# The last two query heads projected inside the first four attention steps

## The chip, the cores and the metric

The kernel runs on one core of one Trainium2 chip. The core has a matrix engine (TensorE, PE in the profile), a vector engine (VectorE, DVE), a scalar engine (ScalarE, ACT), a general engine (GpSimd, POOL) and an engine that here only issues DMA transfers (SyncE, SP). Each runs its own list of instructions in order, and they wait for each other by semaphores. The metric is the device time of one execution in microseconds (us); lower is better.

## The reference

Two layers over a batch of 8 sequences of 112 rows and width 1024, with a context of 375 rows for each sequence. Only the second layer's attention matters here. All of it is float32.

```python
x = x + attention0(layernorm(x), ctx)          # single head, 1024 wide
x = x + ffn0(layernorm(x))                      # routed low-rank experts
# second layer: grouped attention, 32 query heads of 128 in 8 groups of 4
q = apply_rope((layernorm(x) @ wq).reshape(8, 112, 32, 128).transpose(0, 2, 1, 3), pos)
k = apply_rope(ctx @ wk ...)                    # 8 key heads
v = ctx @ wv ...                                # 8 value heads
attn = softmax(q @ k.T / sqrt(128) + mask)
x = x + (attn @ v).reshape(8, 112, 4096) @ wo
x = x + ffn1(layernorm(x))
```

## The kernel before

Every float32 product is made of three TensorE passes over operands that were split into a high and a low part (`split_product`, L202 in the rows). ACT makes the high part, POOL or DVE subtracts it from the raw data to get the low part.

The kernel is a row of phases, each one a block with its own list for every engine, and a block ends with a barrier of all engines. Two phases matter.

**The query phase** (`query1_phase`, from L1071) projects the 32 query heads in 16 pairs. A pair has 4 units (head t of 0 and 1, half h of the 896 tokens). A unit is 24 matmuls of 128x448 into one PSUM bank. DVE then rotates it by the position tables: three products that read the bank (L736 to L738) and one addition of two buffers in SBUF (L1209, into `q_rotated_then_x_rows`), and SP stores it to memory. The weights of the next pair are loaded (L1126), split by ACT (L1162) and by POOL (L1180) in two slots. Units are counted from 0 to 63; the last pair has 60 to 63. Between these last four units stand the first pieces of the attention: the scores of step 0, their masking, exponentials and normalisation. The mask (1312.5 KB) and the first tiles (q and k of steps 0 and 1, v of step 0) are loaded by SP in front of weights of the last pair. A q tile has 224 KB, k 188, v 187.5, a head's weights 512, so this burst has 2836 KB.

**The attention phase** (`attention_phase`, from L1392) has 64 steps, one for each group of 4 heads and each sequence (step s, sequence u = s mod 8, group g = s div 8), written out one after the other. In step s the engines do:

- PE: scores of step s+1 for heads 0 and 1 (6 matmuls), 12 transposes of the normalised scores of step s (L1564), output projection of an earlier step, first half (`project`, 12 matmuls), scores of step s+1 for heads 2 and 3, second half of the projection (12 matmuls), and the product with v (9 matmuls). The projections of steps 0 to 3 don't exist: nothing is finished yet.
- DVE: masks and row maxima of heads 0 and 1 of step s+1 (L1343, L1347), low parts of the three transposed tiles (L1515), the first addition to `y_t` (L1505), masks of heads 2 and 3, the second addition, reciprocal and four scalings (`normalise`, L1360 and L1363, SBUF to SBUF), low part of the output (L1527, `e_o_t_low`).
- ACT: high parts of q and k of step s+2, of the three transposed tiles, exponentials of step s+1, high part of v of step s+1 (L1313), high part of the output (L1461).
- POOL: low parts of q and k of step s+2 (L1319), of v of step s+1 (L1324), in the first half of each group the low part of a tile of the output weights (L1481), and in steps 0 to 3 a memset of a quarter of `y_t` (L1484).

The order on each engine is written by hand. PE starts the transposes of a step only when DVE has normalised that step (`normed`), and `project` of step s waits for the low part of the output of step s - u mod 4 - 1 (`o_low`).

The last phase (`final_phase`) loads 1084 KB of constants and five rows tiles of 448 KB, each issued by SP behind the last v tile.

## Time and profile before

| | |
|---|---|
| Median of 3 runs | 1939.86 us (1935.42 to 1948.66) |
| The profiled execution, whole time | 1937.03 us |
| Its span from the first to the last instruction | 1935.2 us |
| Mean granted TensorE clock | 0.985 of full speed |
| PE busy | 1852.1 us, 96% |
| DVE busy | 1105.3 us, 57% |
| ACT and POOL busy | 627.5 and 622.7 us, 32% each |

Times in the rows are us from the start of the span. "Busy" of PE counts a matmul that runs at a lower clock for its full length. A row with x4 is four instructions merged, with the time from the start of the first to the end of the last.

### The profile page before, as it was taken

How to read it: one execution, taken by the hardware profiler on the slowest of the kernel's cores; microseconds unless marked ns; L12 is line 12 of the kernel's file. 1: busy time of each engine (PE TensorE's matmuls, PEld its weight loads, DVE VectorE, ACT ScalarE, POOL GpSimd, SP SyncE). 2: the span in 40 equal slices, each digit the busy share in tenths (PEclk: the TensorE clock that was granted, in tenths of full speed). 3: DMA queues.
4: the chain of work that ended last, by engine and by line, in shares of the span. 5: the costliest groups of instructions: out<-in, count | busy, mean ns of one | idle time of the engine just before them, and what ended most of it. 6: DMA issues, size and time to landing. Idle time of an engine off the chain costs nothing. (4 is left out here: it accounts for less than half of the span.)

```text
span 1935.2 us, 27961 instructions
## 1 busy us (share of the span) xinstructions
PE 1852.1 (96%) x9628; PEld 1666.0 (86%) x9628; DVE 1105.3 (57%) x2473; ACT 627.5 (32%) x1337; POOL 622.7 (32%) x427
## 2 busy tenths in 40 slices
PE   5999999999999999989999998799999999999996
PEld 5998999998677777768999997699999999999984
DVE  6631465554222222235666665877777777777766
ACT  2211211112222222221111112656666566665612
POOL 2323432225222222212222222634434344343413
PEclk9999999999999999999999999899999999999999
DMA  4112432345333333312222224333323233233403
GB/s 121 55 55 76 146 110 91 99 142 150 118 115 114 114 114 113 100 53 85 98 101 98 102 99 143 96 84 86 99 74 97 84 86 99 74 97 84 126 10 96
DMA packets 137965, 188.98 MB, mean 98 GB/s; under 512 B 41320, under 2 KB 107432, under 8 KB 137872
## 3 DMA queue, kind: packets, MB, share of 16 engines
q1 hardware_dynamic: 137872, 187.80, 31.6%
q8 instruction: 52, 0.85, 0.2%
q14 instruction: 41, 0.34, 0.1%
HBM read 141.14 MB, written 46.63 MB: 97 GB/s over the span
## 5 line engine op out<-in xcount | busy, mean ns | idle before, releaser
L202 PE MATMUL bank<-shared_operand_high,w_first_high 128*128 128x448 f32 (+1 forms) x768 | 279.5, 364 | 15.8 <-issue 4.8
L202 PE MATMUL bank<-shared_operand_high,w_first_low 128*128 128x448 f32 (+1 forms) x768 | 278.8, 363 | 0.0
L202 PE MATMUL bank<-shared_operand_low,w_first_high 128*128 128x448 f32 (+1 forms) x768 | 278.7, 363 | 0.0
L1354 ACT ACTIVATE e_scores<-e_scores,e_nmax 112x375 f32<-112x375 f32 x256 | 155.0, 610 | 126.1 <-DVE e_nmax L1347 120.9
L202 PE MATMUL bank<-e_o_t_high,e_wo_high 128*128 128x448 f32 x512 | 192.5, 376 | 1.3 <-DVE e_o_t_low L1527 1.3
L202 PE MATMUL bank<-e_o_t_high,e_wo_low 128*128 128x448 f32 x512 | 187.3, 366 | 0.0
L202 PE MATMUL bank<-e_o_t_low,e_wo_high 128*128 128x448 f32 x512 | 186.7, 365 | 0.0
L279 POOL TENSOR_TENSOR shared_operand_low<-ctx_raw,shared_operand_high 128x752 fp32r<-128x752 f32 x64 | 116.4, 1831 | 210.3 <-ACT shared_operand_high L275 210.3
L202 PEld LDWEIGHTS bank<-shared_operand_high,w_first_high 128*128 128x128 f32 x768 | 145.9, 190 | 27.9 <-issue 5.3
L202 PEld LDWEIGHTS bank<-shared_operand_low,w_first_high 128*128 128x128 f32 x768 | 145.9, 190 | 9.7
L202 PEld LDWEIGHTS bank<-shared_operand_high,w_first_low 128*128 128x128 f32 x768 | 145.7, 190 | 9.8
L1343 DVE CUSTOM_DVE_ANT_0 e_scores<-bank,e_mask 112x375 f32<-112x375 f32 x256 | 139.9, 546 | 12.1 <-PE bank L202 3.0
L1180 POOL TENSOR_TENSOR w_first_low<-aw_weights_then_ctx_rows,w_first_high 128x1024 fp32r<-128x1024 f32 x30 | 72.4, 2414 | 224.4 <-ACT w_first_high L1162 224.4
L1505 DVE TENSOR_TENSOR y_t<-bank,y_t 128x448 f32<-128x448 f32 x128 | 80.0, 625 | 107.3 <-PE bank L202 107.2
L1324 POOL TENSOR_TENSOR e_v_low<-e_raw_v,e_v_high 125x384 fp32r<-125x384 f32 x64 | 65.1, 1017 | 235.6 <-ACT e_v_high L1313 235.6
L202 PE MATMUL bank<-shared_operand_high,w_rest_low 128*128 128x376 f32 x384 | 128.5, 335 | 0.0
L202 PE MATMUL bank<-shared_operand_low,w_rest_high 128*128 128x376 f32 x384 | 128.4, 334 | 0.0
L202 PE MATMUL bank<-shared_operand_high,w_rest_high 128*128 128x376 f32 x384 | 127.9, 333 | 0.2 <-POOL w_rest_low L677 0.2
L275 ACT ACTIVATE shared_operand_high<-ctx_raw 128x752 fp32r<-128x752 f32 x64 | 52.2, 829 | 219.6 <-DMA ctx_raw<-in_ctx_t 201.1
L1162 ACT ACTIVATE w_first_high<-aw_weights_then_ctx_rows 128x1024 fp32r<-128x1024 f32 x30 | 31.8, 1061 | 261.3 <-PE bank L202 242.2
L202 PE MATMUL bank<-w_rest_high,shared_operand_high 128*125 128x512 f32 x288 | 114.2, 396 | 0.0
L202 PE MATMUL bank<-w_rest_low,shared_operand_high 128*125 128x512 f32 x288 | 113.7, 395 | 0.0
(173 smaller groups left out, 4214.8 us busy)
## 6 DMA issues: line engine op xcount, KB each, us to landing
ctx_raw<-in_ctx_t SPq DMA_DIRECT2D x64, 376.0 KB, 3.7
e_raw_wo<-in_wo SPq DMA_DIRECT2D x32, 512.0 KB, 5.5
aw_weights_then_ctx_rows<-in_wq SPq DMA_DIRECT2D x30, 512.0 KB, 3.6
q_rotated<-q_rotated_then_x_rows SPq DMA_DIRECT2D x64, 224.0 KB, 1.9
e_raw_q<-q_rotated SPq DMA_DIRECT2D x64, 224.0 KB, 2.8
k_rotated<-k_rotated_sb SPq DMA_DIRECT2D x64, 188.0 KB, 1.9
e_raw_k<-k_rotated SPq DMA_DIRECT2D x64, 188.0 KB, 2.9
aw_weights_then_ctx_rows<-in_ctx_nat SPq DMA_DIRECT2D x8, 1500.0 KB
```

Of the source, the lines that this page charges most:

```text
L202: mm = pe.matmul(out, stationary[a], moving[b], start=(first and i == 0), stop=(last and i == 2))
L275: act.activation(k.ctx_ring[0][slot][:, 2 * j:2 * j + 2, :], k.c_raw[:, j % 2], ACT.Copy).then_inc(done, 1)
L279: pool.tensor_tensor(k.ctx_ring[1][slot][:, 2 * j:2 * j + 2, :], k.c_raw[:, j % 2], f32(k.ctx_ring[0][slot][:, 2 * j:2 * j + 2, :]), ALU.s ...
L1162: act.activation(k.w_first[0][:, t], k.raw[:, t], ACT.Copy).then_inc(w_high, 1)
L1180: pool.tensor_tensor(k.w_first[1][:, t], k.raw[:, t], f32(k.w_first[0][:, t]), ALU.subtract).then_inc(w_low, 1)
L1324: pool.tensor_tensor(self.v[1][:, t], self.raw_v[:, t], f32(self.v[0][:, t]), ALU.subtract).then_inc(self.v_low, 1)
L1343: dve.tensor_tensor_reduce(self.s_buf[:, t, h, :], self.s_bank[h % 2][0:SEQ, 0:KEYS], self.mask[:, u, :], 1.0, LOWEST, ALU.add, ALU.max, s ...
L1354: act.activation(self.s_buf[:, t, h, :], self.s_buf[:, t, h, :], ACT.Exp, bias=self.nm[:, t, h:h + 1], accum_out=self.total[:, t, h:h + 1] ...
L1505: dve.tensor_tensor(k.yt[:, tile, at:at + HALF], y_bank[t][:, 0:HALF], k.yt[:, tile, at:at + HALF], ALU.add).then_inc(y_added, 1)
```

## The change

1. The query phase and the attention phase are one block. The barrier between them is gone. Since buffers of both phases now live at the same time, their places in SBUF are laid out by hand: the attention's buffers lie over those of the query phase in an order that lets each be free when it is needed, and the buffers of the last phase (`ln4`, `lora1`, `tri1_sb`) are carved out of the mask's region.
2. The pair loops end one pair earlier. The pieces of attention step 0 now stand between the units of pair 14 (units 56 to 59). The units 60 to 63 are projected one in each of the attention steps 0 to 3, in two halves of 12 matmuls, in the places where later steps have the output projection. Their banks are the two of the output projection. DVE rotates such a unit at the end of the step, after `normalise` and ahead of the low part of the output. SP stores it in the next step.
3. The split of the weights of the last pair moves: the high part of tile 0 goes ahead of the exponentials of step 0, that of tile 1 behind them, and both low parts behind the first q, k and v splits on POOL.
4. The mask is loaded after the first pair's stores, and the first q, k and v tiles one pair earlier, behind the weights.
5. The output weights of group 0 are split in steps 3 to 6 and not 0 to 3. The memsets of `y_t` are gone; the additions of steps 4 to 11 are copies.
6. The loads of the last phase's constants and rows wait until all masks have been read (`first.masked` at 256).

```diff
-            query1_phase(nc, k, first)
-            layer0.close()
-            attention_phase(nc, k, first)
+            with nc.Block() as block:
+                last_heads = query1_phase(nc, k, first, layer0, heads, block)
+                layer0.close()
+                attention_phase(nc, k, first, last_heads, heads, block)
...
+    def bank_of(i, t, h):
+        return bank[2 + h] if known(i) and i == LAST else bank[2 * t + h]
...
+        for unit, (t, h) in enumerate(FIRST):
+            store(unit, 0, t, h)
+        first.load_mask(sp)
...
+        first.split_high(act)
+        weight_high(LAST, 0, 4 * LAST + 2)
+        first.exps(act, 0, 0, range(PER_GROUP))
+        weight_high(LAST, 1, 4 * LAST + 4)
...
+        first.split_low(pool)
+        weight_low(LAST, 0)
+        weight_low(LAST, 1)
...
+    def products_of_last(pe, n, part):
+        if part == 0:
+            pe.wait_ge(w_low, 2 * LAST + n // 2 + 3)
+            pe.wait_ge(read, 4 * LAST + n + 3)
+            products(pe, LAST, n // 2, n % 2, range(CH // 2))
+        else:
+            products(pe, LAST, n // 2, n % 2, range(CH // 2, CH)).then_inc(acc, 1)
...
+            if s < FILLED:
+                last_heads.rotate(dve, s)
+            dve.wait_ge(o_high, s + 1)
...
+            if s < FILLED:
+                last_heads.products(pe, s, 0)
+            else:
+                project(s, u, 0)
...
     @block.sync
     def _(sp):
+        sp.wait_ge(first.masked, 4 * GROUPS * BATCH)
         for dst, src in ((aw, k.a1), (tri, k.tri1)):
```

**The order on PE** at the start of step 0. Before (`e_q` and `e_k` are the split q and k of a step, `e_p_t` the transposed probabilities):

```order
L1564 MATMUL bank<-ident,e_scores 125x112 x12
L202 MATMUL bank<-e_k_high,e_q_high 112x376
L202 MATMUL bank<-e_k_low,e_q_high 112x376
L202 MATMUL bank<-e_k_high,e_q_low 112x376
L202 MATMUL bank<-e_k_high,e_q_high 112x376
L202 MATMUL bank<-e_k_low,e_q_high 112x376
L202 MATMUL bank<-e_k_high,e_q_low 112x376
L202 MATMUL bank<-e_p_t_high,e_v_high 128x448
```

Now (`shared_operand` is the normalised input, `w_first` the query weights):

```order
L1660 MATMUL bank<-ident,e_scores 125x112 x12
L203 MATMUL bank<-shared_operand_high,w_first_high 128x448
L203 MATMUL bank<-shared_operand_low,w_first_high 128x448
L203 MATMUL bank<-shared_operand_high,w_first_low 128x448
L203 MATMUL bank<-shared_operand_high,w_first_high 128x448
L203 MATMUL bank<-shared_operand_low,w_first_high 128x448
```

Twelve projection matmuls stand between the transposes and the next scores, and twelve more behind those scores.

**The order on DVE** at the end of step 0. Before:

```order
L1360 RECIPROCAL e_inv<-e_total 112x4
L1363 TENSOR_SCALAR e_scores<-e_scores,e_inv 112x375 x4
L1527 TENSOR_TENSOR e_o_t_low<-bank,e_o_t_high 128x4x112
L1343 ISA e_scores,e_max<-bank,e_mask 112x375
L1343 ISA e_max 112x1
```

Now:

```order
L1417 RECIPROCAL e_inv<-e_total 112x4
L1420 TENSOR_SCALAR e_scores<-e_scores,e_inv 112x375 x4
L738 TENSOR_TENSOR q_straight<-bank,q_rope 128x448
L739 TENSOR_TENSOR q_crossed<-bank,q_rope 64x448
L740 TENSOR_TENSOR q_crossed<-bank,q_rope 64x448
L1211 TENSOR_TENSOR q_rotated_then_x_rows<-q_straight,q_crossed 128x448
L1620 TENSOR_TENSOR e_o_t_first_low<-bank,e_o_t_first_high 128x4x112
L1400 ISA e_scores,e_max<-bank,e_mask_then_layer_ffn 112x375
```

The four operations of the rotation stand between the scaling of one step and the first mask of the next.

**The order on SP** where the loop over pairs ends. Before:

```order
L1140 COMPARE_AND_BRANCH
L1368 DMA e_mask<-in_mask 112x8x375
L1288 DMA e_raw_q<-q_rotated 128x4x112
L1291 DMA e_raw_k<-k_rotated 128x376
L1288 DMA e_raw_q<-q_rotated 128x4x112
L1291 DMA e_raw_k<-k_rotated 128x376
L1296 DMA e_raw_v<-v_rows 125x3x128
L1126 DMA raw_weights_then_ctx_rows<-in_wq 128x1024
```

Now:

```order
L1130 COMPARE_AND_BRANCH
L1122 DMA raw_weights_then_ctx_rows<-in_wq 128x1024
L1345 DMA e_raw_q<-q_rotated 128x4x112
L1348 DMA e_raw_k<-k_rotated 128x376
L1345 DMA e_raw_q<-q_rotated 128x4x112
L1348 DMA e_raw_k<-k_rotated 128x376
L1353 DMA e_raw_v<-v_rows 125x3x128
L1116 DMA q_rotated<-q_rotated_then_x_rows 128x448 x2
```

The weights stand first, and the mask is not in this place at all.

## Rows read from the trace of the kernel before

**Rows 1.** The page, busy time of PE: us, share, instructions.

```profile
PE 1852.1 (96%) x9628; PEld 1666.0 (86%) x9628; DVE 1105.3 (57%) x2473; ACT 627.5 (32%) x1337; POOL 622.7 (32%) x427
```

**Rows 2.** Waits of PE, 1150 to 1265: total us, times, longest.

```profile
PE bank L1564 <- DVE e_scores L1363: 12.8, 4, 5.2
PE bank L202 <- PEq L1075: 3.5, 1, 3.5
PE bank L202 <- POOL w_first_low L1180: 2.9, 1, 2.9
PE bank L202 <- POOL e_k_low L1319: 0.7, 1, 0.7
```

**Rows 3.** Windows: length, busy PE, PEld, DVE, ACT, POOL, granted clock, DMA.

```profile
1202.00:1248.00 46.00, 31.91 (x147) 29.38 (x147) 38.11 (x86) 28.63 (x67) 25.62 (x19) 0.78 0.41 115
```

**Rows 4.** Timeline of PE, last query units to step 4: start, length.

```profile
1173.91 0.37 PE L202 MATMUL bank<-shared_operand_high,w_first_low 128*128 128x448 f32 x1
...
1182.19 0.34 PE L202 MATMUL bank<-e_k_high,e_q_high 128*112 128x376 f32 x1
...
1183.21 0.37 PE L202 MATMUL bank<-shared_operand_high,w_first_high 128*128 128x448 f32 x1
...
1248.37 0.45 PE L202 MATMUL bank<-e_o_t_high,e_wo_high 128*128 128x448 f32 x1
```

**Rows 5.** Timeline of PE, transposes of two later steps.

```profile
1257.20 1.46 PE L1564 MATMUL bank<-ident,e_scores 112*125 112x112 f32 x12
...
1267.29 1.46 PE L1564 MATMUL bank<-ident,e_scores 112*125 112x112 f32 x12
```

**Rows 6.** Timeline of DVE, attention steps 0 to 2.

```profile
1209.32 0.15 DVE L1347 TENSOR_SCALAR e_nmax<-e_max 112x1 f32<-112x1 f32 x1
...
1210.46 2.12 DVE L1363 TENSOR_SCALAR e_scores<-e_scores,e_inv 112x375 f32<-112x375 f32 x4
...
1213.03 0.53 DVE L1343 CUSTOM_DVE_ANT_0 e_scores<-bank,e_mask 112x375 f32<-112x375 f32 x1
...
1217.66 0.15 DVE L1347 TENSOR_SCALAR e_nmax<-e_max 112x1 f32<-112x1 f32 x1
...
1218.80 6.89 DVE L1363 TENSOR_SCALAR e_scores<-e_scores,e_inv 112x375 f32<-112x375 f32 x4
```

**Rows 7.** Timeline of DVE, the last query pair: rotation and scaling.

```profile
1184.37 1.13 DVE L1209 TENSOR_TENSOR q_rotated_then_x_rows<-q_straight,q_crossed 128x448 f32<-128x448 f32 x1
...
1194.26 0.62 DVE L736 TENSOR_TENSOR q_straight<-bank,q_rope 128x448 f32<-128x448 f32 x1 [1.92 <-PE bank L202]
...
1196.93 1.39 DVE L1363 TENSOR_SCALAR e_scores<-e_scores,e_inv 112x375 f32<-112x375 f32 x4
```

**Rows 8.** Timeline of POOL beside those DVE operations.

```profile
1184.03 1.00 POOL L1319 TENSOR_TENSOR e_k_low<-e_raw_k,e_k_high 128x376 fp32r<-128x376 f32 x1
...
1210.70 1.02 POOL L1324 TENSOR_TENSOR e_v_low<-e_raw_v,e_v_high 125x384 fp32r<-125x384 f32 x1 [5.45 <-ACT e_v_high L1313]
...
1220.42 2.34 POOL L1481 TENSOR_TENSOR e_wo_low<-e_raw_wo,e_wo_high 128x1024 fp32r<-128x1024 f32 x1
```

**Rows 9.** Timeline of SP (issues) and ACT: mask, weights of pairs 2 and 15.

```profile
906.75 0.35 SPq L1126 DMA_DIRECT2D aw_weights_then_ctx_rows<-in_wq  x1
...
921.39 1.06 ACT L1162 ACTIVATE w_first_high<-aw_weights_then_ctx_rows 128x1024 fp32r<-128x1024 f32 x1 [8.67 <-PE bank L202]
...
1159.71 0.36 SPq L1368 DMA_DIRECT2D e_mask<-in_mask  x1
...
1173.68 1.06 ACT L1162 ACTIVATE w_first_high<-aw_weights_then_ctx_rows 128x1024 fp32r<-128x1024 f32 x1 [17.76 <-DMA aw_weights_then_ctx_rows<-in_wq]
```

**Rows 10.** Timeline of SP and DVE around the start of the last phase.

```profile
1820.23 0.51 SPq L1626 DMA_DIRECT2D a_sb<-in_a  x1
...
1837.64 0.15 DVE L1347 TENSOR_SCALAR e_nmax<-e_max 112x1 f32<-112x1 f32 x1
...
1856.64 1.28 DVE L1686 TENSOR_TENSOR q_rotated_then_x_rows<-bank,q_rotated_then_x_rows 112x512 f32<-112x512 f32 x2
```

More of the change, by code:

```diff
@@ L1263, in __init__ @@
         self.v = pair("e_v", [KEY_TILE, 2, KEY_TILES, P])
-        self.mask = sb("e_mask", [SEQ, BATCH, KEYS])
+        self.mask_region = sb("e_mask_then_layer1_ffn", [P, BATCH * KEYS])
+        self.mask = self.mask_region[0:SEQ, :].rearrange("q (b s) -> q b s", b=BATCH)
         self.s_buf = sb("e_scores", [SEQ, 2, H, KEYS])
@@ L1380, in split_high @@
         self.qk_high_part(act, 1, 1)
-        self.exps(act, 0, 0, range(PER_GROUP))
     def split_low(self, pool):
@@ L1591, in final_phase, with step @@
-def final_phase(nc, k, first, sb, sem, block, y_added, y_of_quad):
+        def step(s, u, g):
+            more = s + 1 < STEPS
+            if more:
+                first.mask_scores(dve, s + 1, (u + 1) % 8, (0, 1))
+            for c in range(KEY_TILES):
+                dve.wait_ge(pt_high, 3 * s + c + 1)
+                dve.tensor_tensor(pt[1][:, c, :], p_bank[c][0:KEY_TILE, 0:HALF], f32(pt[0][:, c, :]),
+                                  ALU.subtract).then_inc(pt_low, 1)
+            if s >= FILLED:
+                add_y(s, u, 0)
+            if more:
+                first.mask_scores(dve, s + 1, (u + 1) % 8, (2, 3))
+            if s >= FILLED:
+                add_y(s, u, 1)
+            if more:
+                first.normalise(dve, s + 1, (u + 1) % 8)
+            if s < FILLED:
+                last_heads.rotate(dve, s)
+            dve.wait_ge(o_high, s + 1)
+            at = (slice(None), slice(None), slice((u % 4) * SEQ, (u % 4 + 1) * SEQ))
+            dve.tensor_tensor(ot[1][u // 4][at], o_bank[:, 0:HALF].rearrange("p (h t) -> p h t", h=H),
+                              f32(ot[0][u // 4][at]), ALU.subtract).then_inc(o_low, 1)
@@ new lines, in carve, with sb, final_phase @@
+def carve(region):
+    used = [0]
+    def sb(name, shape):
+        size = math.prod(shape[1:])
+        at = used[0]
+        used[0] = at + size
+        flat = region[0:shape[0], at:at + size]
+        if len(shape) == 3:
+            return flat.rearrange("p (a b) -> p a b", a=shape[1])
+        if len(shape) == 4:
+            return flat.rearrange("p (a b c) -> p a b c", a=shape[1], b=shape[2])
+        return flat
+    return sb
+def final_phase(nc, k, first, sem, block, y_added, y_of_quad):
@@ L1601, in final_phase @@
     xr, spare = first.rows[0:SEQ], first.s_buf
+    sb = carve(first.mask_region)
     ln = NormBuffers(sb, "ln4", 2)
-    xnt = sb("xn4_t", [P, 2, CH, SEQ])
+    xnt = k.xn4_t
     lora = LoraBuffers(sb, "lora1", L1_EXPERTS)
-    aw, bw = sb("a1_sb", [P, CH, width]), sb("b1_sb", [L1_EXPERTS * RANK, DIM])
+    aw, bw = k.a1_sb, k.b1_sb
     tri = sb("tri1_sb", [SEQ, L1_EXPERTS, L1_EXPERTS])
```

654 lines of the change are left out of this document (348 added, 306 removed).

## The prediction

> **What bounds the kernel now.** I read the page first. PE is busy 96% of the span [rows 1], so only time that PE idles, or runs at a lower clock, can be won. The list of PE's waits between 1150 and 1265 us holds what this change touches: 12.8 us for the scaled scores (DVE, L1363), 3.5 us at the block's end, 2.9 us for the last pair's weights, 0.7 us for the low part of k, in all 19.9 us [rows 2]. The windows say what stands beside it: from 1202 to 1248 PE is busy 31.9 of 46 us, at a mean granted clock of 0.78 [rows 3]. So part of the stretch ran at 1.2 GHz and not at 2.4, after PE had idled.
>
> The chain of waits has DVE's four scalings as its longest piece in steps 1 to 3. With nothing to project, PE has about half of a step's work there, and each step waits for the softmax of the next. One scaling of four heads took 2.12 us in one step and 6.89 us in the next [rows 6], against 1.39 us where POOL rests [rows 7]. In those stretches POOL was running a low part [rows 8]. Two things bound steps 0 to 3: too little PE work, and DVE behind POOL.
>
> **The stretch, measured.** Unit 59 ends at 1173.91 + 0.37 = 1174.28. The first output projection, in step 4, starts at 1248.37 [rows 4]. That is 74.1 us, and everything large in the change lies in it. A full step takes 1267.29 - 1257.20 = 10.09 us [rows 5]. The four units of 24 matmuls of 128x448 fill the places of the 24 projection matmuls of the same size, so four full steps hold both the units and steps 0 to 3.
>
> With no waits and full clock the stretch would be: two score pairs of step 0 (1183.21 - 1182.19 = 1.02 each [rows 4]), 2.04; four steps, 40.36; the scores and transposes of step 4, 1.02 + 1.23 (an estimate from the 1.46 us row less the overlap of the last matmul). Sum 44.65 us. So the ideal gain is 74.1 - 44.65 = 29.4 us: 19.9 of idle, and 9.5 that must be the lower clock.
>
> **What comes back as new waits.**
>
> 1. *The first scores of step 0 wait for POOL.* PE does them right after unit 56. POOL can make the low parts of q and k only behind the weight split that starts at the end of unit 55: ACT 1.06 [rows 9], POOL 2.3 (the output weights' split has the same shape [rows 8]), q and k at 1.0 to 1.15 each [rows 8]: 5.5 us. A unit takes half of 8.67 + 1.06 [rows 9], 4.87. PE waits 0.7 us. Bounds: 0 and the 2.9 us of [rows 2].
>
> 2. *DVE becomes the pace of steps 0 to 3.* I take its round in the step that has no unit: from the last row maximum at 1209.32 to the same at 1217.66, 8.34 us [rows 6]. In it nothing but exponentials (ACT) and scores is waited for. The rotation adds four operations of 0.62 [rows 7], 2.5 us: 10.84. PE's own pace is 10.09, so PE would idle 0.75 us in each step. The 8.34 holds one collision: the scaling took 2.12 in place of 1.39, with POOL's v split at 1210.70 beside it [rows 6 to 8]. The split of v starts when the exponentials end, in the new kernel too, so I keep it. Without it the round would be 10.1, exactly PE's.
>
> 3. *The rotation brings a second collision.* Its addition reads two buffers in SBUF, and beside POOL's split of k it took 1.13 and not 0.62 [rows 7, 8]. In the new order POOL splits q and k (2.1 us together) about where the scaling ends and the addition comes. I take one such loss of 0.5 in each round: 11.35. The bounds are 10.1 (no collision at all, PE paces) and 12.0 (a scaling also waits for the whole of a 1.15 us split).
>
> The Trainium skill (SBUF — State Buffer, Who interferes with whom) says that a vector operation in a 2-port mode, or with two SBUF inputs against a GpSimd operation that reads SBUF, blocks fully until the other is done. This speaks against the change, since the addition is such an operation and now lies in DVE's round. By it alone the round would be near the upper bound, 12.0, and the time 1916; the 1.13 us row agrees in kind.
>
> 4. *Step 4 waits for the low part of step 3's output,* which stands behind the last rotation.
>
> Working, with E the end of unit 59. First scaling (step 1's) done: rotation of unit 59 beside the last weight split 3.0, masks and low parts up to the last maximum 1217.66 - 1213.03 = 4.63, from there to the end of the scaling 1212.58 - 1209.32 = 3.26 [rows 6]: E + 10.9. Three rounds of 11.35: E + 45.0. Rotation 2.5 and the low part 0.5: E + 48.0, where the output projection starts. The whole stretch is 2.04 + 0.7 + 48.0 = 50.7 us. Gain 74.1 - 50.7 = 23.4 us.
>
> The same at the bounds. PE paces: its transposes of step 4 start at E + 41.4; with the rotation and low part of 3.0 behind, the projection starts at E + 44.4, the stretch is 47.1, the gain 27.0. Rounds of 12.0: E + 10.9 + 36.0 + 3.5 = E + 50.4, gain 21.0. In the bad case PE idles 1.9 us in each step. The four gaps of before, 3.2 us on average [rows 2], went with 9.5 us of low clock; shorter ones may bring back part of that, at most all of it.
>
> **Edits costed at nothing, and their cover.**
>
> - The early mask. Its 1312.5 KB now go ahead of pair 2's weights (512 KB) at 906.75. The burst of before, 2836 KB from 1159.71 to 1173.68 [rows 9], ran at 203 KB/us; so the weights land 9.0 us later, at 915.8, and ACT and POOL are done at 919.3. PE needs them at 921.4, when unit 7 ends [rows 9]. Cover 2 us; without it one wait of PE, and at most some 5 us.
> - The late weights of the last pair. The mask is out of their way, and they stand ahead of the tiles: the 2.9 us wait goes (it is in the 19.9).
> - The last phase's loads now wait for the last mask, 1837.64, not 1820.23: 17.4 us later [rows 10]. 3.3 MB at the rate above need 16 us: 1854, and the first row, behind 1.1 MB of constants, is there by about 1846. DVE reads it at 1856.64 [rows 10]. Cover 10 us. On SP nothing is queued behind this wait but these loads.
> - The store of a unit stands in SP's queue behind the next q, k and v loads and waits for the rotation. The load behind it is for three steps ahead. The first loads after unit 59 wait for its store, some 5 us into step 0, and are needed at the end of it.
> - The split of group 0's output weights in steps 3 to 6 is 1.06 on ACT ahead of the exponentials, where ACT waits for maxima; memsets and additions were off PE's path except through POOL's 6.89 us collision, which steps 0 to 2 can't have any more.
> - The barrier: 3.5 us, in the 19.9.
>
> **The time.** 1937.0 - 23.4 = 1913.7, so **1914 us**. The profiled execution stands 2.8 us under the median of the three runs, inside their spread of 13; I add nothing to the forecast, and a little to the upper end.
>
> **The rivals.**
>
> *A. No collisions, PE paces all steps* (for: in full steps the scaling took its short time, as PE's even 10.09 shows [rows 5]; against: there a second addition to y delays the scaling past the split of v). 1910.
>
> *B. Heavy collisions and some low clock.* The round is 12 or more and PE's gaps pull the clock down for a part of the stretch. Gain 21.0 less 3 to 9.5: 1919 to 1925. For: 6.89 us once [rows 6]. Against: POOL's long runs (output weights, memset, q, k in one piece) are broken up.
>
> *C. Slower: the clock stays at 1.2 GHz through steps 0 to 3.* One mechanism: the gaps at the start of each step, 1.3 us and more, hold the granted clock low, and 40.4 us of PE work take twice as long. Then the stretch is some 50.7 + 37 us, and the time 1951. It ends slower once the low clock takes 23 of these 40 us. Against: with 20 us of idle, the old stretch lost only 9.5. The Trainium skill (TensorE: Matmul & The Clock Gate, What's actually happening) says that the clock depends on how busy the engine has been; with PE over 85% busy in every step that rule is on the forecast's side.
>
> *D. The change does not do what it says: something in the shared layout or the moved loads holds a step up.* Either the mask's burst or a q tile that waits for the store of unit 59. Each would eat 5 to 15 us once: 1919 to 1929.
>
> **How the numbers follow.** Forecast (round 10.6 to 11.7, 1911 to 1917): 0.50. A: 0.20. B: 0.16. D: 0.10. C: 0.04. The range leaves out C and most of D and the fastest of A: 1907 to 1925. About 1% (19 us) is what a measurement of this kernel can tell from no change. Faster by over 1% is below 1920: forecast and A, most of whose lower ends stay under it (0.66 with some loss for the spread of the runs), and a third of B and D, 0.06: 0.72. Slower by over 1%: C and a rest, 0.04. Within 1%: 0.24.
>
> **What would show it.** In the profile of the changed kernel:
>
> - PE's wait for the block's end and the one for the weights of the last pair are gone; a short one (0.7) for the low part of k stands after unit 56.
> - Between transposes of steps 0 to 4 lie 11 to 11.5 us, not 10.1, each with a wait of about 1.3 for the scaled scores (L1420), and a wait of about 2 for the low part of the output at step 4's projection. If the spacing is 10.1, A is right; if 12 or more, B.
> - The scaling takes about 2.1 us in these steps, the addition L1211 over 0.62 in some.
> - The granted clock is 1.00 or close to it from unit 56 to step 4.
> - The stretch from the end of unit 59 to step 4's projection, with the scores of step 0 in front, is 51 us against 74.
>
> The prediction is wrong if PE waits in these steps for something else than DVE's scaling, if the clock falls, or if the last phase waits for its rows.

## The result and the profile after

The changed kernel takes 1918.67 us (median of 4 runs, 1914.39 to 1921.2), the kernel before 1944.0 us beside it. The ratio is 0.9872, 95% interval 0.9828 to 0.9917: faster by 1.3%, and by 0.8% at least. The profiled execution took 1921.2 us, against 1937.03 before.

The page of the changed kernel, span and busy time as in [rows 1]:

```profile
span 1919.4 us, 27912 instructions
PE 1854.2 (97%) x9628; PEld 1662.2 (87%) x9628; DVE 1098.9 (57%) x2473; ACT 627.6 (33%) x1337; POOL 616.8 (32%) x423
```

PE's work is the same, its busy share rose from 96% to 97%. The waits of PE from 1150 to 1265, which answer to [rows 2]:

```profile
PE bank L203 <- DVE e_o_t_first_low L1620: 1.4, 1, 1.4
PE bank L203 <- POOL e_k_low L1376: 1.1, 1, 1.1
PE bank L1660 <- DVE e_scores L1420: 1.0, 4, 0.3
```

19.9 us of listed waits became 3.5. The block's end and the weights of the last pair are no longer in the list, and the four waits for scaled scores are 1.0 together, not 12.8.

The windows of the changed kernel, steps 0 to 3, then the 20 us in which the first output projection begins (columns as in [rows 3]):

```profile
1184.00:1231.00 47.00, 44.78 (x250) 40.43 (x248) 41.98 (x104) 29.05 (x68) 19.79 (x16) 1.00 0.42 116
1220.00:1240.00 20.00, 18.31 (x90) 16.48 (x89) 16.03 (x46) 10.87 (x26) 8.95 (x6) 0.91 0.34 102
```

Over steps 0 to 3 PE is busy 44.8 of 47 us at a granted clock of 1.00, against 31.9 of 46 at 0.78 [rows 3]. Behind the wait of 1.4 us the clock falls for 3.4 us. PE's timeline there and at the start of the stretch, to be read with [rows 4]:

```profile
1184.30 0.36 PE L203 MATMUL bank<-shared_operand_high,w_first_low 128*128 128x448 f32 x1
...
1231.20 0.47 PE L203 MATMUL bank<-e_o_t_first_high,e_wo_first_high 128*128 128x448 f32 x1 [1.44 <-DVE e_o_t_first_low L1620]
...
1232.16 0.57 PE L203 MATMUL bank<-e_o_t_first_high,e_wo_first_high 128*128 128x448 f32 x1
1232.53 0.57 PE L203 MATMUL bank<-e_o_t_first_low,e_wo_first_high 128*128 128x448 f32 x1
```

From the end of unit 59 (1184.30 + 0.36) to the projection are 46.5 us. The last two lines start 0.37 us apart: that is the level of 1.2 GHz, where 0.20 is usual at 2.4 GHz.

DVE's timeline in step 0, beside [rows 6, 7]:

```profile
1193.04 0.15 DVE L1404 TENSOR_SCALAR e_nmax<-e_max 112x1 f32<-112x1 f32 x1
...
1194.17 2.16 DVE L1420 TENSOR_SCALAR e_scores<-e_scores,e_inv 112x375 f32<-112x375 f32 x4
1196.25 0.61 DVE L738 TENSOR_TENSOR q_straight<-bank,q_rope 128x448 f32<-128x448 f32 x1
...
1198.16 0.63 DVE L1211 TENSOR_TENSOR q_rotated_then_x_rows<-q_straight,q_crossed 128x448 f32<-128x448 f32 x1
...
1203.63 0.15 DVE L1404 TENSOR_SCALAR e_nmax<-e_max 112x1 f32<-112x1 f32 x1
```

and POOL's beside it, as [rows 8]:

```profile
1194.42 1.04 POOL L1381 TENSOR_TENSOR e_v_low<-e_raw_v,e_v_high 125x384 fp32r<-125x384 f32 x1 [3.67 <-ACT e_v_high L1370]
1196.21 1.14 POOL L1376 TENSOR_TENSOR e_q_low<-e_raw_q,e_q_high 128x448 fp32r<-128x448 f32 x1 [0.75 <-ACT e_q_high L1361]
1197.31 0.99 POOL L1376 TENSOR_TENSOR e_k_low<-e_raw_k,e_k_high 128x376 fp32r<-128x376 f32 x1
```

The round is 1203.63 - 1193.04 = 10.59 us, in each of the steps. The scaling takes 2.16 beside the split of v. The rotation's operations that read a bank run at their usual 0.6 us beside the splits of q and k, and the addition, which reads two buffers, starts 0.14 us before the split of k ends and keeps its 0.63.

**Where the 15.8 us between the two spans are.** I cut both traces at the first matmul of unit 56 and at the transposes of step 6; between the cuts stands the same work in both.

| | first matmul of unit 56 | from there to transposes of step 6 | from there to the end |
|---|---|---|---|
| before | 1154.65 | 112.6 | 667.9 |
| after | 1161.44 | 90.3 | 667.7 |

The middle gained 22.4 us. The part in front lost 6.8, although its work hardly differs. The first unit starts 1.5 us later, and from there to unit 56 it takes 280.4 us and not 275.1: the 128x448 matmuls of the changed kernel start 206.7 ns apart and those of the kernel before 202.7 (the mean over units 8 to 55), both at a granted clock of 1.00. Whether the change causes that was the first question for the chip.

### The profile page after: what moved, and what is told of

It is laid out like the page before. It is cut to its first block, busy times and chain, and to the rows that moved or that the text cites. A ratio compares the mean times of both kernels' runs of the same rounds, so it can differ in the third digit from the quotient of the medians.

```text
span 1919.4 us, 27912 instructions
## 1 busy us (share of the span) xinstructions
PE 1854.2 (97%) x9628; PEld 1662.2 (87%) x9628; DVE 1098.9 (57%) x2473; ACT 627.6 (33%) x1337; POOL 616.8 (32%) x423
## 4 chain that ended last, share of the span: by engine, by line
PE 34%; issue 14%; DVE 3%; POOL 2%; DMA 0%; ACT 0%; POOLq 0%; DVEq 0%; ACTq 0%
PE bank L203 29%; PE bank L1660 4%; POOL w_first_low L1186 2%; PE bank L183 1%; DVE e_scores L1420 0%; DVE e_scores L1400 0%; PE bank L100 0%; DVE e_p_t_low L1606 0%; DMA q_rotated_then_x_rows<-x_after_layer 0%; DVE e_mask_then_layer_ffn L91 0%; DVE q_crossed L740 0%; DVE q_crossed L739 0%; DMA out<-q_rotated_then_x_rows 0%; DVE e_mask_then_layer_ffn L173 0%; POOL q_rotated_then_x_rows L1796 0%
## 5 line engine op out<-in xcount | busy, mean ns | idle before, releaser
L203 PEld LDWEIGHTS bank<-shared_operand_high,w_first_low 128*128 128x128 f32 x768 | 146.3, 191 | 11.8
L1400 DVE CUSTOM_DVE_ANT_0 e_scores<-bank,e_mask_then_layer_ffn 112x375 f32<-112x375 f32 x256 | 139.8, 546 | 9.6 <-PE bank L203 0.4
L1597 DVE TENSOR_TENSOR y_t<-bank,y_t 128x448 f32<-128x448 f32 x112 | 69.9, 624 | 93.9 <-PE bank L203 93.8
L203 PE MATMUL bank<-w_rest_high,shared_operand_low 128*125 128x512 f32 x288 | 113.6, 394 | 0.0
L1606 DVE TENSOR_TENSOR e_p_t_low<-bank,e_p_t_high 125x448 fp32r<-125x448 f32 x192 | 107.5, 616 | 5.9 <-ACT e_p_t_high L1543 5.9
L882 ACT ACTIVATE v_out<-bank 125x512 f32<-125x512 f32 x48 | 28.7, 597 | 209.8 <-PE bank L203 209.8
```

Source lines behind the costliest of these rows:

```text
L203: mm = pe.matmul(out, stationary[a], moving[b], start=(first and i == 0), stop=(last and i == 2))
L882: act.activation(v_out[:, p % 2], v_bank[p % 2][0:KEY_TILE, :], ACT.Copy).then_inc(v_read, 1)
L1400: dve.tensor_tensor_reduce(self.s_buf[:, t, h, :], self.s_bank[h % 2][0:SEQ, 0:KEYS], self.mask[:, u, :], 1.0, LOWEST, ALU.add, ALU.max, s ...
L1597: dve.tensor_tensor(k.yt[:, tile, at:at + HALF], y_bank[t][:, 0:HALF], k.yt[:, tile, at:at + HALF], ALU.add).then_inc(y_added, 1)
L1606: dve.tensor_tensor(pt[1][:, c, :], p_bank[c][0:KEY_TILE, 0:HALF], f32(pt[0][:, c, :]), ALU.subtract).then_inc(pt_low, 1)
```

## The experiments

My theory: the gain is PE's idle time and low clock in steps 0 to 3, filled by the units; what is left over the ideal is DVE's round, lengthened where POOL holds it up. The rivals: that other parts (barrier, mask, copies) bring it; that the round of 10.6 has another cause. Every distance from unit 56 to step 6 below is taken as in the table.

**1 and 2. Both kernels again.** No edit.

> The changed kernel unchanged. What it tells is the spacing of matmuls of 128x448 in the query phase. In the one execution of after that I have, it is 206.7 ns from 888 us to the end of unit 57; in that of before it is 202.6 ns over the same units (except unit 61). That costs about 5.6 us, the whole of what separates the stretch's gain of 24.4 us from the measured 18.7 or so less two small terms. Theory R (the level is drawn anew in each execution or by a small shift of time): this execution may have 202.6 ns over some of the units, and then its time is up to 6 us shorter, about 1914 us. Theory C (the change's code sets it): 206.7 ns again over all of them, 1919 us. The ratio to before should come out near 0.988 either way.

> The kernel before unchanged, one look, for the spacing of its 128x448 matmuls in the query phase. Theory R: other units than unit 61 may have 206.7 ns this time, up to 6 us longer in all. Theory C: 202.6 ns again over units 0 to 57, about 1937 us.

Measured: 1913.12 us (5 runs, 1911.76 to 1917.77), ratio 0.9869 (0.9847 to 0.9891); the kernel before 1938.19 in its one run, 1939.4 over the runs of that chip. First a window of the query phase in the first execution of the changed kernel:

```profile
900.00:1100.00 200.00, 200.00 (x969) 181.66 (x968) 129.77 (x163) 21.22 (x20) 50.23 (x21) 1.00 0.32 105
```

Then, of the second execution, the stretch at the projection and the same window:

```profile
1220.00:1240.00 20.00, 18.32 (x103) 16.97 (x103) 16.26 (x46) 12.90 (x31) 10.33 (x8) 1.00 0.46 127
900.00:1100.00 200.00, 200.00 (x989) 185.39 (x988) 130.41 (x165) 22.29 (x21) 50.48 (x21) 1.00 0.32 106
```

The same code put 989 matmuls in 200 us, not 969: 202.7 ns apart. So the change does not fix the pace; theory C fell. Behind the same wait for the output's low part (1.46 us) the clock stayed at 1.00 this time, and from step 4's transposes to step 5's it took 11.94 us and not 13.43. With both executions at 202.7 ns the sum closes: the kernel before took 112.2 us from unit 56 to step 6, the changed one 88.7, a gain of 23.5; 2.5 in front and 0.2 behind make 26.2, the difference of the spans (1936.4 and 1910.2). The 2.5 in front can't be credited to the change: the first unit starts at 881.0 and 878.4 us in these two, and anywhere from 877.5 to 882.5 in the thirteen traces of this case.

**3. The low part ahead of the rotation.**

```diff
-            if s < FILLED:
-                last_heads.rotate(dve, s)
             dve.wait_ge(o_high, s + 1)
...
                               f32(ot[0][u // 4][at]), ALU.subtract).then_inc(o_low, 1)
+            if s < FILLED:
+                last_heads.rotate(dve, s)
```

> The changed kernel with one order turned round on VectorE in steps 0 to 3: the low part of a step's output comes ahead of the rotation of the unit, not behind it. My theory: step 4's output projection waited 1.4 us because step 3's low part stood behind the last rotation (2.5 us), and TensorE's granted clock fell behind that wait (0.91 mean from 1220 to 1240). Turned round, the low part starts when ScalarE has the high part, so the wait goes (to 0.3 or less), and with it the low clock: 1.4 to 3.5 us less than the changed kernel, 1915.5 to 1917.5 where that has 1919. The round of the steps stays at 10.6 us. Rival: VectorE now waits for ScalarE's high part in each step, which delays the rotation and the next row maximum, the round grows to 11 us or more, and the gain is 0 or below (1919 to 1922).

Measured: 1916.85 us (6 runs, 1912.01 to 1925.04), ratio 0.9893 (0.9867 to 0.9919). The waits of PE, 1140 to 1265:

```profile
PE bank L1660 <- DVE e_scores L1420: 2.6, 5, 1.7
PE bank L203 <- POOL e_k_low L1376: 1.2, 1, 1.2
```

The wait for the low part is gone, and one of 1.7 us for step 5's scaled scores has come. DVE's scaling for step 5, then POOL's splits beside it:

```profile
1232.51 3.03 DVE L1420 TENSOR_SCALAR e_scores<-e_scores,e_inv 112x375 f32<-112x375 f32 x4
```

```profile
1232.76 1.05 POOL L1381 TENSOR_TENSOR e_v_low<-e_raw_v,e_v_high 125x384 fp32r<-125x384 f32 x1 [3.96 <-ACT e_v_high L1370]
1234.03 1.30 POOL L1376 TENSOR_TENSOR e_q_low<-e_raw_q,e_q_high 128x448 fp32r<-128x448 f32 x1 [0.22 <-ACT e_q_high L1361]
```

Behind step 4's transposes this scaling starts 0.7 us sooner than in the second execution of the changed kernel, but it now meets the splits of v and q and takes 3.03 us, where it took 1.74 there. The round is 10.59 as before, 89.2 us from unit 56 to step 6 against 88.7. The gain was nil, as the rival had it, but by another way: a wait of about the same size came back behind the projection, from a new collision. The clock stayed at 1.00 behind it.

**4. The high part of v between the exponentials.**

```diff
                 first.exps(act, s + 1, (u + 1) % 8, (0, 1))
+                if s < FILLED:
+                    first.v_high_part(act, s + 1, (u + 1) % 8)
                 first.exps(act, s + 1, (u + 1) % 8, (2, 3))
-                first.v_high_part(act, s + 1, (u + 1) % 8)
+                if s >= FILLED:
+                    first.v_high_part(act, s + 1, (u + 1) % 8)
```

> The changed kernel with ScalarE's high part of v between the exponentials of heads 0, 1 and those of heads 2, 3 in steps 0 to 3, so that GpSimd's low part of v runs some 1.5 us earlier than VectorE's scaling of the scores. My theory: the round of 10.6 us in these steps is 10.1 (what TensorE needs) plus a part of the collision, in which the scaling takes 2.15 us and not 1.39 beside the v split. With the split out of the way the scaling takes about 1.4, the round is 10.1, and the kernel is about 2 us faster (4 rounds of 0.5), 1917 where the changed kernel has 1919. Rival 1: the exponentials of heads 2, 3 come later by the 0.3 to 0.5 us of the high part and take all of it back, 1919. Rival 2: the split now lies beside the reciprocal or row sums and some other operation is stretched instead, 1919 to 1921.

Measured: 1913.03 us (4 runs), ratio 0.9866 (0.9842 to 0.989), beside 1913.12 of the changed kernel on the same chip; 88.7 us from unit 56 to step 6, no gain. DVE's timeline:

```profile
1197.89 1.39 DVE L1420 TENSOR_SCALAR e_scores<-e_scores,e_inv 112x375 f32<-112x375 f32 x4
...
1201.11 1.36 DVE L1211 TENSOR_TENSOR q_rotated_then_x_rows<-q_straight,q_crossed 128x448 f32<-128x448 f32 x1
```

and POOL's:

```profile
1195.11 1.02 POOL L1381 TENSOR_TENSOR e_v_low<-e_raw_v,e_v_high 125x384 fp32r<-125x384 f32 x1 [3.67 <-ACT e_v_high L1370]
...
1200.99 1.01 POOL L1376 TENSOR_TENSOR e_k_low<-e_raw_k,e_k_high 128x376 fp32r<-128x376 f32 x1
```

The scaling got its 0.76 us back, so DVE was a little earlier, so its addition began 0.12 us after the split of k, not near its end, and took 1.36 and not 0.63. That is rival 2 in its outcome, the loss is the same and has moved, though the operation that it met is the split of k and not that of v. PE shows no wait for scaled scores here, yet the transposes still stand 10.6 us apart; the time sits in the gaps between score matmuls, which wait for a bank until DVE has masked it. PE's wait for the output's low part at step 4 is 1.9 us here, and the clock stayed at 1.00 behind it.

**5. No filling.** All of the change, but the last four units are projected and rotated in one piece ahead of step 0.

```diff
         rotated_half(dve, unit + 3, LAST - 1, 1, 1)
+        for n in range(4):
+            rotate_last(dve, n)
...
         half_tile(unit + 3, LAST - 1, 1, 1)
+        for n in range(4):
+            products_of_last(pe, n, 0)
+            products_of_last(pe, n, 1)
...
-            if s < FILLED:
-                last_heads.products(pe, s, 0)
-            else:
+            if s >= FILLED:
                 project(s, u, 0)
```

> The changed kernel, but units 60 to 63 are projected right behind unit 59 and steps 0 to 3 hold no projection; all else of the change stays (one block, early mask, copies in place of memsets and additions, no barrier). My theory: the filling itself is most of the gain, since each of the four steps is paced by VectorE's round (8.3 to 8.5 us without a rotation) and TensorE has only some 5.2 us of work in it. The stretch from the first scores of step 0 to step 4's projection is 2.7 + 19.5 + 34 + 2.4 = 59 us at full clock, up to 67 if the clock falls to 1.2 GHz again in the steps, against 50 in the changed kernel: 1922 to 1930 us in all. Rival: the collisions with the memsets, the barrier and the mask were what made the old stretch long, and filling adds little; then the time is within 5 us of the changed kernel (1913 to 1918). The granted clock from step 0 to 3 tells whether TensorE's idle gaps alone bring the low clock (0.75 to 0.83 in the kernel before).

Measured: 1934.63 us (10 runs, 1927.39 to 1942.28), ratio 0.9968 (0.9943 to 0.9993); 104.1 us from unit 56 to step 6. The window of steps 1 to 4:

```profile
1200.00:1240.00 40.00, 26.82 (x131) 23.92 (x131) 35.79 (x87) 24.14 (x61) 15.52 (x13) 0.87 0.34 99
```

By the traces filling is worth 104.1 - 88.7 = 15.3 of the 23.5 us, two thirds, and the rival fell. The trace is that of the fastest of the ten runs, though, and by medians filling is worth more: this kernel lies 7.5 us below the 1942.11 of the kernel before on the same chip, and the changed kernel 25 to 28 below its own in three sets. The median also lies outside the 1922 to 1930 that I expected, and only the profiled 1927.39 inside. The remaining 8 us of the traces, for barrier, mask, weights and copies together, were not taken apart in the changed kernel. With gaps of 2.7 to 4.0 us PE's clock went to a mean of 0.87, with no barrier and no memset. My rounds were too short: 9.7 to 10.9 us, not 8.3 to 8.5, since each scaling took 3.7 us. DVE and POOL in one step:

```profile
1206.30 3.72 DVE L1425 TENSOR_SCALAR e_scores<-e_scores,e_inv 112x375 f32<-112x375 f32 x4
```

```profile
1206.54 1.02 POOL L1386 TENSOR_TENSOR e_v_low<-e_raw_v,e_v_high 125x384 fp32r<-125x384 f32 x1 [21.59 <-ACT e_v_high L1375]
1207.53 1.24 POOL L1381 TENSOR_TENSOR e_q_low<-e_raw_q,e_q_high 128x448 fp32r<-128x448 f32 x1
1208.72 1.09 POOL L1381 TENSOR_TENSOR e_k_low<-e_raw_k,e_k_high 128x376 fp32r<-128x376 f32 x1
```

Without PE work between them, the splits of v, q and k come in one piece, and the four instructions of the scaling end 0.2 us behind the last. So filling does two things: it gives PE work, and it spreads POOL's work over the step.

**6. The copies alone, in the kernel before.**

```diff
-                if known(s) and s < 4:
-                    pool.memset(k.yt[:, 2 * s:2 * s + 2, :], 0.0).then_inc(y_zeroed, 1)
...
+                if s < 12:
+                    dve.tensor_copy(k.yt[:, tile, at:at + HALF], y_bank[t][:, 0:HALF]).then_inc(y_added, 1)
```

> The kernel before with one part of the change alone: no memsets of the output tiles on GpSimd in steps 0 to 3, and copies in place of additions in steps 4 to 11. My theory: the scaling of 6.89 us in step 2 (and 5.8 in step 3) is VectorE kept out while GpSimd runs output-weight split, memset and the low parts in one piece; without the memsets it falls to some 2 to 4 us. The rounds of 13.1 and 12.4 us become 9 to 11, which gives 4 to 9 us: 1930 to 1935 against 1939 for the kernel before. Rival: the memsets only stood beside it, the splits alone hold VectorE as long, and the time is 1938 to 1940.

Measured: 1934.07 us (10 runs), ratio 0.998 (0.9957 to 1.0002), beside 1942.11 before. From unit 56 to step 6 it is 111.4 us, where the two traces of the kernel before have 112.6 and 112.2. The long scalings, DVE's timeline of this kernel:

```profile
1217.40 4.22 DVE L1363 TENSOR_SCALAR e_scores<-e_scores,e_inv 112x375 f32<-112x375 f32 x4
...
1236.49 4.22 DVE L1363 TENSOR_SCALAR e_scores<-e_scores,e_inv 112x375 f32<-112x375 f32 x4
```

The scalings for steps 1 to 4 took 2.12, 6.89, 5.76 and 2.15 us before and take 2.13, 4.22, 2.15 and 4.22 here: the two long ones fell, near what I expected (2 to 4), and the last one rose. The rounds are 8.5 to 10.2 us. But 3 us came back behind them: PE waited 4.5 us for the second 4.22, its clock fell, and from step 4's transposes to step 5's it took 13.3 us, at a clock of 0.75 in that window, where the kernel before took 10.2. What stayed is 1 us in the traces and 8 in the medians, with an interval of the ratio that includes 1: at the lower edge of what a measurement can tell.

**7. The early mask alone, in the kernel before.**

```diff
             for unit, (t, h) in enumerate(FIRST):
                 store(unit, 0, t, h)
+            first.load_mask(sp)
...
     def load(self, sp):
-        sp.dma_start(self.mask[:, :, :], self.k.mask.rearrange("b q s -> q b s")).then_inc(self.mask_in, 16)
```

> The kernel before with one part of the change alone: the mask (1312 KB) is loaded at the start of the query phase, behind the stores of the first pair, and not in the burst at the end. My theory: the 2.9 us wait of TensorE for the last pair's weights goes to 0 to 0.5, as does nothing else: 1936 to 1937 against 1939. Rival 1: the q, k and v tiles of step 0 are loaded sooner too and nothing waits for them, so the gain is the same 2.9 or less. Rival 2: the early mask delays pair 2's weights, a new wait of up to 5 us at 921, and the time is 1938 to 1942.

Measured: 1941.6 us (10 runs), ratio 1.0001 (0.9979 to 1.0024). PE's waits from 850 to 1290, two lines:

```profile
PE bank L1567 <- DVE e_scores L1364: 16.1, 4, 5.1
...
PE bank L202 <- PEq L1075: 3.5, 1, 3.5
```

The 2.9 us wait for weights is gone, and the waits for the scaled scores rose from 12.8 to 16.1: the scalings of steps 2 to 4 took 5.77, 5.75 and 5.77 us in place of 6.89, 5.76 and 2.15. From unit 56 to step 6 it is 116.3 us, 4 more, although step 0's transposes came 1.6 us sooner (48.2 us behind the start of unit 56, not 49.8). The shift put one more scaling beside a long run of POOL. None of my three expectations was that. No wait for pair 2's weights appeared, so the time of rival 2 was met without its mechanism.

**8. Both reorderings of 3 and 4.**

> The changed kernel with both reorderings in steps 0 to 3: the high part of v between the exponentials, and the low part of the output ahead of the rotation. With the first alone the scaling took 1.39 and not 2.15 us, but the rotation's addition then started inside GpSimd's split of k and took 1.36 to 1.40 in place of 0.62, so the round stayed at 10.6: the collision had only moved. With both, the addition starts some 0.6 us later, where at most 0.2 us of that split are left. My theory: neither operation is stretched, VectorE's round is about 9.9 to 10.05, TensorE paces the steps at 10.1, and the distance from the end of unit 59 to step 6's transposes falls from 65.5 us to about 63.5: some 2 us faster than the changed kernel (1911 where that has 1913). Rival: the waiting of a VectorE operation for GpSimd moves once more, to another operation of the round, which stays at 10.6, 1913.

Measured: 1913.3 us (6 runs), ratio 0.9867 (0.9836 to 0.9897). DVE's timeline:

```profile
1198.41 1.39 DVE L1420 TENSOR_SCALAR e_scores<-e_scores,e_inv 112x375 f32<-112x375 f32 x4
...
1202.43 0.63 DVE L1211 TENSOR_TENSOR q_rotated_then_x_rows<-q_straight,q_crossed 128x448 f32<-128x448 f32 x1
```

Neither is stretched, PE's waits list nothing in steps 0 to 3, and from step 1 to step 4 the transposes stand 10.05 to 10.09 us apart: the round of 10.6 was PE's 10.09 plus the rest of one collision. From the end of unit 59 to step 6 it is 64.0 us, where the changed kernel takes 65.5 and I expected 63.5. At the end of the filled steps one wait of 1.7 us is left, since step 5's scaling takes 3.02 us beside the splits of v and q, as in experiment 3. The gain of 1.5 us stands in the trace alone; the medians (1913.3 here, 1913.12 of the changed kernel on another chip) don't show it.

**9. The changed kernel a third time.** No edit.

> The changed kernel unchanged, a third execution with a trace, next to the two variants of this call. So far one execution of it had 206.7 ns between its 128x448 matmuls over all of units 0 to 57 and a lower clock behind the 1.4 us wait at step 4; the next had 202.5 ns and a clock of 1.00 behind the same wait. If both are drawn per execution, nothing binds them together, and this one may show either; the likeliest is 202.5 ns (nine of ten traces) and a time near 1913 us. If it shows 206.7 again, then the level depends on the kernel too, with a chance of its own.

Measured: 1916.39 us (6 runs), ratio 0.986 (0.9833 to 0.9886). The six are 1910.1, 1912.2, 1913.1 and 1919.6, 1920.5, 1922.3: two groups. The profiled one (1920.5) has 206.7 ns again in units 0 to 57, and behind the wait at step 4 the clock of 0.91 and 13.45 us to step 5. That is 7.2 us more up to unit 56 than in the second execution (5.2 of them between the first unit and unit 56) and 1.5 more behind it. Of the three traced executions of this kernel two had 206.7 ns, of the ten of the other kernels here none in all units. So the change does not fix the pace, but that it raises the chance of 206.7 ns is not excluded; 5 us would then be a price of the change that the forecast does not have.

**10. The early v in step 4 too.** The edit is against the version of experiment 8.

```diff
                 first.exps(act, s + 1, (u + 1) % 8, (0, 1))
-                if s < FILLED:
+                if known(s) and s <= FILLED:
                     first.v_high_part(act, s + 1, (u + 1) % 8)
```

> The version with both reorderings, and ScalarE's early high part of v in step 4 too. In that version the steps were paced by TensorE (10.09 us), but a wait of 1.7 us was left ahead of step 5's transposes: the scaling there took 3.02 us, since the v split (at 1229.80) and behind it the q split (1231.05) began while it ran. My theory: with the v split made earlier, the scaling is 1.39 to 1.45 and the wait falls to 0.2 or less, the distance from step 4's to step 5's transposes from 12.27 to about 10.6, and the whole from the start of unit 56 to step 6's transposes from 88.0 to about 86.4 us; the time is 1911 to 1912. Rival: the q split alone, which begins when the output's high part is made, still holds the scaling (2.1 us), the wait is 0.8 to 1, and half of the gain is lost.

Measured: 1914.02 us (5 runs, 1904.84 to 1916.12), ratio 0.9848 (0.9822 to 0.9874). PE's waits, 850 to 1290, all but the end of the phase before:

```profile
PE bank L203 <- POOL e_k_low L1376: 1.2, 1, 1.2
```

The scaling of step 5 takes 1.39 us, the wait is gone, steps 4 to 5 take 10.63 us, and 85.6 us lie between unit 56 and step 6, 3.2 less than the changed kernel's 88.7. Against the version of experiment 8 it is 1.7 less, where I expected 1.6 (its distance is 87.2; the 88.0 in the expectation was counted from four matmuls too early, and the 86.4 with it). The profiled execution is the fastest of all, 1904.8 us; the median is 2 us above the 1911 to 1912 expected. By the medians of the same chip (1914.0 and 1916.4, overlapping intervals) that is not told apart from the changed kernel; that it is better rests on the trace alone.

**11. The split of v made twice.** The low part of v is written twice in steps 0 to 3 (the values stay); PE is told after the second.

```diff
+            if s < FILLED:
+                first.v_low_part(pool, s + 1, (u + 1) % 8, False)
+                pool.wait_ge(first.v_once, s + 1)
             if s + 1 < STEPS:
                 first.v_low_part(pool, s + 1, (u + 1) % 8)
```

> The changed kernel with GpSimd's low part of v made twice in steps 0 to 3 (the same values written again; TensorE is told after the second). It stands for a second GpSimd operation of 1.0 us behind the first, as the memset of the output tiles (1.59 us) would be. My theory: while GpSimd runs such an operation, no instruction of VectorE's scaling runs, one can slip in between two of them; so the scaling takes 2.15 + 0.85 = 3.0 us in each of the four steps, VectorE's round is 11.4 and not 10.6, and TensorE waits some 1 us for the scaled scores: 3.3 us slower in all, 1916.5 where the changed kernel has 1913. Rival: the loss in the round has another source (the rotation, the order of the operations), the second split finds VectorE at work that reads a bank, and the time stays at 1913.

Measured: 1924.57 us (4 runs, 1919.19 to 1927.89), ratio 0.9912 (0.9885 to 0.9939), 8 us above the changed kernel on the same chip. DVE and POOL in step 0:

```profile
1184.98 3.79 DVE L1422 TENSOR_SCALAR e_scores<-e_scores,e_inv 112x375 f32<-112x375 f32 x4
```

```profile
1185.22 2.13 POOL L1382 TENSOR_TENSOR e_v_low<-e_raw_v,e_v_high 125x384 fp32r<-125x384 f32 x2 [3.66 <-ACT e_v_high L1371]
1187.31 1.24 POOL L1377 TENSOR_TENSOR e_q_low<-e_raw_q,e_q_high 128x448 fp32r<-128x448 f32 x1
1188.51 1.09 POOL L1377 TENSOR_TENSOR e_k_low<-e_raw_k,e_k_high 128x376 fp32r<-128x376 f32 x1
```

The mechanism holds and I had its size too small. Here and in step 2 the second split fills the 0.75 us pause ahead of the split of q, and the scaling is held for that too (3.79 and 3.77 us); in steps 1 and 3 it takes the 2.9 that I expected, and the addition is stretched instead (0.98 and 1.03 us). The rounds are 11.8 to 12.6 us, the distance from unit 56 to step 6 is 95.2 us, 6.5 more for one operation of 1 us per step. PE's clock was 0.91 from 1180 to 1220, which is a part of it. That the copies in place of memsets are worth about as much here is argued and not shown: a memset of 1.59 us behind the split of v would stand in the same place. The memset itself was not tried in the changed kernel, where `y_t` lies over buffers still in use.

## Why the prediction was right

Predicted 1914 (1907 to 1925), measured 1918.67, 1913.12 and 1916.39 in three sets. The forecast's mechanism held: DVE paces steps 0 to 3, the collision of the scaling stays, PE waits a little in each step and once at step 4's projection. One of its own signs of being wrong was met all the same, a fall of the clock, in two executions of three and at a cost of 1.5 us. The forecast was counted from the profiled 1937.0 of the kernel before, which is fast for it: its medians beside the three sets are 1944.0, 1939.4 and 1944.56. As a difference of medians the gain is thus 25.3, 26.3 and 28.2 us, more than the 23.4 of the sum. Point by point:

- **The new wait for the low part of k**: 0.7 predicted, 1.1 to 1.2 measured. In the first execution POOL's split of q took 1.54 us and not 1.15, beside a rotation's addition of 2.02: the collision stretches both.
- **To the end of the first scaling**: E + 10.9 predicted, 1196.33 - 1184.66 = 11.7 measured. The rotation of unit 59 took 4.1 and not 3.0: its addition beside the weight split took 2.14, a loss of 1.5 where I had put 0.5.
- **The round**: 11.35 predicted, 10.6 measured; three of them make -2.3 us. This is the term that was mis-sized, and with it PE's wait for the scaled scores in each step, 1.3 predicted and 0.3 measured. The rest of its sum was right: 8.34 + 2.5 = 10.84, less 0.24, since from the first mask to the last maximum DVE took 4.39 us (1199.24 to 1203.63) and not the 4.63 of [rows 6], which lie in the stretch with the low clock [rows 3]. The second collision, which I took as given, was absent: the three products of the rotation (1.9 us) last nearly as long as the splits of q and k (2.1), so that the addition starts only 0.14 us before the end of the split of k and is not stretched. Experiment 4 moved DVE by 0.76 us and the collision appeared, at 0.73 us and not my 0.5; experiment 8 moved it again and it was gone. So rival A's condition, no collisions, was met by experiments 8 and 10 alone, and there PE paced at 10.09 as A has it.
- **Rotation and low part ahead of step 4**: 3.0 predicted, 1231.20 - 1228.13 = 3.1 measured. The wait of PE was 1.4 to 1.5, not 2.
- **The sum**: projection at E + 46.5, not 48.0; stretch 49.7, not 50.7 (2.04 + 1.1 + 46.5); gain in it 24.4, not 23.4. The errors of the terms are +0.4, +0.8, -2.3 and +0.1, and only their sum is as small as 1.0: that the total came so close is in part luck.
- **The clock**: 1.00 up to the projection, as forecast. Behind the wait of 1.4 us it fell in two executions of three, and cost 1.5 us. I had counted no loss there. Rival C's mechanism did not occur with gaps of 0.3 us; it is real with larger ones (0.87 with gaps of 2.7 to 4.0 us in experiment 5).
- **Edits costed at nothing**: the early mask, the late weights, the last phase's loads and the stores brought no new wait; from step 6 to the end all three executions take 667.6 to 667.8 us, where the kernel before took 667.9 and 668.0. The forecast let the memsets reach PE only by the scaling of 6.89 us. Experiments 6 and 11 bear that out and widen it: a POOL operation behind the split of v holds the scaling, and without memsets those of 6.89 and 5.76 us fell to 4.22 and 2.15, though a later one rose from 2.15 to 4.22.
- **Rivals B and D**: no execution of the changed kernel showed a round of 12 or a wait for the mask or the stores.

The first profiled execution lies 7.2 us above the forecast although the stretch gained 1.0 more. What stands against that was not in the sum: the pace of the matmuls in the query phase (5.3), its start 1.5 us later, and the clock behind step 4 (1.5). The one traced execution of this kernel that shows neither pace nor clock took 1911.95 us.

The Trainium skill (SBUF — State Buffer, Who interferes with whom) says that of a vector operation in a 2-port mode and a GpSimd operation, the one that issues first keeps the shared ports for the whole instruction, and the other is blocked until then. The traces agree, and add the price: a scaling of four instructions takes 1.39 us alone and 2.15 beside one split, and beside several operations it ends 0.2 us behind the one that it last waited for (3.72 with three splits, 4.22 with v and the output weights, 5.76 with a memset behind those). In experiment 11 one instruction of the scaling gets in behind each POOL operation; that is not always so, as one instruction of the scaling of 5.76 us took 4.02 us and stayed out for the split of the output weights and the memset together.

Not settled: what draws 206.7 or 202.7 ns, whether the changed kernel draws 206.7 more often than others, and what decides whether the clock falls behind such a wait. Pace and low clock came together in two executions of the changed kernel and were both absent in the third, but the low clock does not need the slow pace: in experiment 11, at 202.7 ns, it followed two waits of 1.9 us and not a third of 1.8.

## What to carry to other kernels

Work of the bound engine that can be moved into stages where it starves is worth its idle time and the clock that the idle time costs: here 15 of 24 us by the traces. Price the engine that then sets the pace instruction by instruction, and each of its operations that POOL can block with both values, since a shift of 0.8 us decided here which applies (experiment 4). Removing one collision may only move it, and parts of such a change need not add: by the traces the mask alone cost 4 us, the copies alone gave 1, and all together with the filling 24. Take the same kernel's trace twice before explaining a few us.

## What the hardware showed unexpectedly

- Back-to-back matmuls of 128x448 at a granted clock of 1.00 start either 202.7 or 206.7 ns apart, for a whole phase of 280 us. It changed between executions of one kernel and is worth 5.2 to 5.3 us here; inside an execution it changed where a set of six 376-column matmuls ran (206.7 in unit 57 and 202.5 in unit 58 of the first execution).
- A POOL memset blocks DVE's scaling as a subtraction does: the 5.76 us scaling of the kernel before ends at 1238.08, 0.2 us after the memset that ends at 1237.88. First its four instructions, shortest, median and longest in ns; the one of 4020 starts at 1234.1, and two of POOL's operations pass before it ends.

```profile
L1363 DVE TENSOR_SCALAR e_scores<-e_scores,e_inv x4: 406/790/4020, 1232.3 to 1234.1; 112x375 f32<-112x375 f32 x4
```

```profile
1232.57 1.04 POOL L1324 TENSOR_TENSOR e_v_low<-e_raw_v,e_v_high 125x384 fp32r<-125x384 f32 x1 [6.04 <-ACT e_v_high L1313]
1233.94 2.40 POOL L1481 TENSOR_TENSOR e_wo_low<-e_raw_wo,e_wo_high 128x1024 fp32r<-128x1024 f32 x1 [0.34 <-ACT e_wo_high L1467]
1236.29 1.59 POOL L1484 MEMSET y_t<- 128x1792 f32 x1
```

- A wait of PE of 1.4 us, after 47 us of near full work, was followed by 1.2 GHz for 3.4 us in two executions and by nothing in a third. Single waits of 1.7 to 1.9 us at step 4's projection or step 5's transposes in experiments 3, 4 and 8 were followed by nothing either.
